# The first batch's output projection moved to the end of the attention block

## The reference, cut to what matters

```python
q, k, v = (xn @ Wq.T + bq) * SCALE, xn @ Wk.T + bk, xn @ Wv.T + bv      # 16 heads of 16
probs = softmax(einsum('bqhd,bkhd->bhqk', q, k))                          # 4096 x 4096 for each head
attn = einsum('bhqk,bkhd->bqhd', probs, v).reshape(b, s, d) @ Wo.T + bo
ffn = sum over 8 experts of weight(xn) * ((silu(xn @ Wg) * (xn @ Wu)) @ Wd)
return x + attn + ffn
```

## Time and profile before

| | us |
|---|---|
| median of three runs | 6645.73 |
| lowest, highest run | 6642.88, 6661.02 |
| the profiled execution's own time | 6664.44 |
| its span | 6662.7 |
| output phase | 6583.84 to 6662.7 |

### The profile page before, as it was taken

One profiled execution on the slowest core, in us unless ns is written; L12 is line 12 of the kernel. 1 busy time (PEld: TensorE's weight loads), 2 busy tenths in 40 slices (PEclk: granted clock), 3 DMA queues, 4 the chain that ended last, 5 costly groups with the idle time before them and its releaser, 6 DMA issues. The chain is left out here.

```text
span 6662.7 us, 158241 instructions
## 1 busy us (share of the span) xinstructions
PE 6493.2 (97%) x57104; PEld 3100.8 (47%) x57104; DVE 5738.7 (86%) x6163; ACT 4968.8 (75%) x9045; POOL 518.2 (8%) x543
## 2 busy tenths in 40 slices
PE   7999999979999999999999999999999999999996
PEld 6888888833333333333333333333333333333334
DVE  4554554479999999999999999999999999999982
ACT  3333333318888888888888888888888888888884
POOL 2222222200000000000000000000000000000000
PEclk9999999969999999999999999999999999999998
DMA  2111111121111111111111111111111111111104
GB/s 94 45 45 45 45 45 45 39 34 26 32 34 33 30 29 29 29 30 29 30 30 29 30 29 30 29 29 29 32 32 32 32 32 33 34 31 29 29 10 159
DMA packets 248804, 248.24 MB, mean 37 GB/s; under 512 B 167848, under 2 KB 208552, under 8 KB 241704
## 3 DMA queue, kind: packets, MB, share of 16 engines
q1 hardware_dynamic: 235872, 202.88, 13.8%
q0 software_dynamic: 12176, 35.14, 2.2%
HBM read 159.26 MB, written 76.58 MB: 35 GB/s over the span
## 5 line engine op out<-in xcount | busy, mean ns | idle before, releaser
L904 DVE TENSOR_REDUCE mx<-sc 128x1 f32<-128x1024 f32 x4096 | 5001.7, 1223 | 91.0 <-PE sc L797 33.4
L891 ACT ACTIVATE pr<-st 128x512 f32<-128x512 f32 x8120 | 4413.8, 597 | 620.8 <-PE st L811 594.4
L820 PE MATMUL pv<-pr,vst 128*32 128x256 f32 x32768 | 2611.8, 391 | 23.3 <-ACT oT L880 15.3
L811 PE MATMUL st<-experts 50*128 50x512 f32 x8120 | 2041.4, 499 | 4.6 <-ACT pr L891 3.0
L797 PE MATMUL sc<-experts 48*128 48x512 f32 x8192 | 1672.4, 405 | 36.4 <-DVE mx L904 27.7
L811 PEld LDWEIGHTS st<-experts 50*128 50x128 f32 x8120 | 757.3, 183 | 1675.5 <-ACT pr L891 1668.7
L820 PEld LDWEIGHTS pv<-pr,vst 128*32 128x32 f32 x32768 | 648.2, 108 | 1545.2 <-ACT pr L891 784.8
L797 PEld LDWEIGHTS sc<-experts 48*128 48x128 f32 x8192 | 788.8, 189 | 77.0 <-DVE mx L904 66.2
L432 ACT ACTIVATE gated<-gate 128x512 f32<-128x512 f32 x256 | 152.2, 599 | 631.2 <-PE up L75 631.0
L602 DVE TENSOR_TENSOR hraw<-gated,up 128x512 f32<-128x512 f32 x256 | 173.2, 686 | 431.2 <-ACT gated L432 428.0
L75 PE MATMUL gate<-xT,experts 128*128 128x512 f32 x1536 | 407.6, 402 | 10.5 <-issue 10.5
(11 more groups left out here) (101 smaller groups left out, 1279.4 us busy)
## 6 DMA issues: line engine op xcount, KB each, us to landing
experts<-parts_d SPq DMA_DIRECT2D x372, 256.0 KB, 4.3
parts_d<-part SPq DMA_DIRECT2D x64, 512.0 KB, 3.0
x_in<-in_L_attn_hidden_states SPq DMA_DIRECT2D x16, 512.0 KB, 4.6
v_d<-v_sb SPq DMA_DIRECT2D x32, 256.0 KB, 2.2
vst<-v_d SPq DMA_DIRECT2D x128, 64.0 KB, 2.2
experts<-turned SPq DMA_DIRECT2D x512, 4.0 KB
sums_d<-oT SPq DMA_DIRECT2D x256, 32.0 KB
whole<-sums_d POOLq DMA_DIRECT2D x32, 256.0 KB, 2.9
```

Source lines behind the costliest of these rows:

```text
L811: nc.tensor.matmul(score_bank(at, x + grp), kr[par][r0:r0 + ROWSM, kb * P:(kb + 1) * P], qr[par][r0:r0 + ROWSM, q0:q0 + GT], start=True, s ...
L820: last = nc.tensor.matmul(pv[VC * j:VC * (j + 1), cols], vst[par][:, kb, :], pr[:, (QSUB * kb + j) % PRING, cols], start=(kb == 0 and half ...
L891: nc.scalar.activation(pr[:, (QSUB * kb + j) % PRING, :], score_bank(2 * at + q, x), ACT.Exp).then_inc(st_read, 1)
L904: nc.vector.reduce_max(mx[par][:, u // MAXU, u % MAXU:u % MAXU + 1], sc[g % 2][:, :], AX.X).then_inc(sc_read, 1)
```

## The change

Groups 0 to 7 of the output, which are the first batch's, are taken inside the attention's block. Groups 8 to 15 stay in the output phase, whose loops now run over 8 groups.

- Loads. In pass 61 (`q == 1`) SP issues 16 loads of 256 KB, the first batch's whole `attn_d`, into a third of the `experts` buffers that the attention does not use. In pass 62 (`q == 2`) it issues 8 loads of 256 KB, the base of groups 0 to 3, into four new `early_base` tiles. Each load waits for a count of `pv_done`, one load for each 1.5 key blocks.
- Compute. Behind the last values' product PE has the 8 groups' matmuls, with `sc` as accumulators; ACT has their high parts behind the last `sums_kept`; DVE has the low parts of groups 0 and 1 ahead of the last head's `inverted`, and the rest behind it. The high and low parts lie in `kept_rows(c, 0)`, the rows of the even heads; the sums of base and product are written to `pr`.
- Stores. Behind the last `sums`, SP waits for each group's sum, reloads `early_base` for groups 4 to 7, and stores the group. SP ends the block when all eight have landed.

The core of the diff, in which the output phase's other loops change in the same way as those shown:

```diff
@@ attention_phase, names
+        o_base = [sb(f"early_base{i}", [P, TPG, D], F32) for i in range(HELD)]
...
+        def o_attn(g):
+            flat = c.experts[g // HELD][:, 2, :, :, :].rearrange("p e k i -> p (e k i)")
+            return flat[:, g % HELD * KC * GT:(g % HELD + 1) * KC * GT].bitcast(F32).rearrange("p (k t) -> p k t", t=GT)
+        def o_attT(g, hl):
+            return kept_rows(c, 0)[g % 2][:, hl * KC * GT:(hl + 1) * KC * GT].rearrange("p (k t) -> p k t", t=GT)
+        def o_out(g):
+            return pr[:, 2 * g:2 * g + 2, :].rearrange("p s (u d) -> p (s u) d", d=D)
@@ sync
+            def early(piece):
+                g, half = divmod(piece, 2)
+                if g < GPB:
+                    sp.dma_start(o_attn(g)[:, half, :], c.attn_d[half * P:(half + 1) * P, g * GT:(g + 1) * GT]).then_inc(o_attn_in, DMA)
+                else:
+                    g -= GPB
+                    sp.dma_start(o_base[g][:, 2 * half:2 * half + 2, :], rows_of(c.base_d, g)[:, 2 * half:2 * half + 2, :]).then_inc(o_base_in, DMA)
...
                     ending = last and q // 2 == heads - 1
+                    if last and q in (1, 2):
+                        sp.wait_ge(attn_stored, H * DMA)
+                        for piece in range(2 * GPB) if q == 1 else range(2 * GPB, 2 * GPB + 2 * HELD):
+                            wait_alone(sp, pv_done, s * KB + PV_PRE + 1 + QK_EVERY * (piece % (2 * GPB)) // 2, passed)
+                            early(piece)
...
             in_turn(body)
+            for g in range(GPB):
+                wait_alone(sp, o_sum, g + 1, passed)
+                if g + HELD < GPB:
+                    sp.dma_start(o_base[g][:, :, :], rows_of(c.base_d, g + HELD)).then_inc(o_base_again[g], DMA)
+                sp.dma_start(rows_of(a["out"], g), o_out(g)).then_inc(o_stored, DMA)
             sp.wait_ge(sums_stored, (SUPERS * SUM_STORES + 1) * DMA)
+            sp.wait_ge(o_stored, GPB * DMA)
@@ tensor
                 times_v(SUPERS - 1, KB - 1, RING - 1, half)
+            for g in range(GPB):
+                pe.wait_ge(o_low, (g + 1) * KC)
+                if g >= 2:
+                    pe.wait_ge(o_sum, g - 1)
+                for t in range(TPG):
+                    last = product(nc, sc[g % 2][:, t * D:(t + 1) * D], [[o_attT(g, hl)[:, k, t * P:(t + 1) * P] for hl in range(2)] for k in range(KC)],
+                                   [[v[:, k, :] for v in c.woT] for k in range(KC)])
+                last.then_inc(o_full, 1)
@@ scalar
             sums_kept(SUPERS - 1)
+            act.wait_ge(o_attn_in, 2 * GPB * DMA)
+            for g in range(GPB):
+                if g >= 2:
+                    act.wait_ge(o_full, g - 1)
+                for k in range(KC):
+                    nc.scalar.activation(o_attT(g, 0)[:, k, :], o_attn(g)[:, k, :], ACT.Identity).then_inc(o_high, 1)
@@ vector
+            early_low(0)
+            early_low(1)
             inverted(HEADS - 1)
+            dve.wait_ge(o_base_in, 2 * HELD * DMA)
+            for g in range(GPB):
+                dve.wait_ge(o_full, g + 1)
+                if g >= HELD:
+                    dve.wait_ge(o_base_again[g - HELD], DMA)
+                for i in range(2):
+                    ins = nc.vector.tensor_tensor(o_out(g)[:, 2 * i:2 * i + 2, :], sc[g % 2][:, i * GT:(i + 1) * GT].rearrange("p (t d) -> p t d", d=D),
+                                                  o_base[g % HELD][:, 2 * i:2 * i + 2, :], ALU.add)
+                ins.then_inc(o_sum, 1)
+                if g + 2 < GPB:
+                    early_low(g + 2)
@@ output_phase, sync
-            for g in range(NG):
-                i, b, c0 = g % DEEP, g // GPB, (g % GPB) * GT
+            for g in range(GPB):
+                i, b, c0 = g % DEEP, 1, g * GT
```

More of the change, by code:

```diff
@@ L40 @@
 RING = 2
+HELD = 4
 ORDER = ((0, 1, 0), (0, 0, 1))
@@ L654, in attention_phase @@
         attn_stored = sem("attn_stored")
+        o_attn_in = sem("early_attn_in")
+        o_base_in = sem("early_base_in")
+        o_base_again = [sem(f"early_base_again{i}") for i in range(HELD)]
+        o_high = sem("early_high")
+        o_low = sem("early_low")
+        o_full = sem("early_full")
+        o_sum = sem("early_sum")
+        o_stored = sem("early_stored")
         passed = sem("passed_a")
@@ L690, in attention_phase, with rows_of @@
         WHEN_IN = {0: (0, 1), UNITS // 2: (2,), UNITS: (3,)}
+        def o_attn(g):
[5 more added lines that the diff above has]
+            return pr[:, 2 * g:2 * g + 2, :].rearrange("p s (u d) -> p (s u) d", d=D)
+        def rows_of(dram, g):
+            return dram[g * GT:(g + 1) * GT, :].rearrange("(t p) d -> p t d", p=P)
         def first_order(g):
@@ L964, in _, with early_low @@
             counted(dve, body)
-            inverted(HEADS - 1)
+            def early_low(g):
+                if g >= 2:
+                    dve.wait_ge(o_full, g - 1)
+                for k in range(KC):
+                    dve.wait_ge(o_high, g * KC + k + 1)
+                    nc.vector.tensor_tensor(o_attT(g, 1)[:, k, :], o_attn(g)[:, k, :], o_attT(g, 0)[:, k, :].bitcast(F32), ALU.subtract).then_inc(o_low, 1)
+            early_low(0)
+            early_low(1)
+            inverted(HEADS - 1)
+            dve.wait_ge(o_base_in, 2 * HELD * DMA)
[9 more added lines that the diff above has]
+                    early_low(g + 2)
 def output_phase(nc, a, c):
@@ L997, in _ @@
                     sp.wait_ge(stored[i], (g // DEEP) * DMA)
-                sp.dma_start(base[i][:, :, :], tokens_of(c.base_d, g)).then_inc(base_in[i], DMA)
+                sp.dma_start(base[i][:, :, :], tokens_of(c.base_d, GPB + g)).then_inc(base_in[i], DMA)
             for i in range(DEEP):
-                sp.wait_ge(stored[i], (NG // DEEP) * DMA)
+                sp.wait_ge(stored[i], (GPB // DEEP) * DMA)
         @block.gpsimd
         def _(pool):
-            for g in range(NG):
+            for g in range(GPB):
                 pool.wait_ge(sum_ready, g + 1)
-                nc.gpsimd.dma_start(tokens_of(a["out"], g), base[g % DEEP][:, :, :]).then_inc(stored[g % DEEP], DMA)
+                nc.gpsimd.dma_start(tokens_of(a["out"], GPB + g), base[g % DEEP][:, :, :]).then_inc(stored[g % DEEP], DMA)
         @block.tensor
         def _(pe):
-            for g in range(NG):
+            for g in range(GPB):
                 pe.wait_ge(low_ready, (g + 1) * KC)
@@ L1038, in _ @@
             low(0)
-            for g in range(NG):
-                if g + 1 < NG:
+            for g in range(GPB):
+                if g + 1 < GPB:
                     low(g + 1)
```

## The result

Five runs of each kernel: the changed one 6622.15 us (median; 6618.49 to 6627.22), the kernel before 6657.05 (6642.88 to 6661.02). The ratio of the two, over all runs, is 0.9959, 95% interval 0.9948 to 0.9969, so about 27 us less, and anything from 21 to 35; the two medians alone differ by 34.9. The forecast had 6622.7 us and 23.1 us less. That the absolute time is hit to 0.6 us is luck. The forecast was taken from the median of three runs of before, 6645.73; from that of all five, 6657.05, the same gain gives 6634.

A forecast was written before the change was run, and what follows sets the result against it. Bounds: the last division with PE idle, POOL's DRAIN at the barrier, then a transfer-limited output phase. Barrier at 6594.65 plus 44.98 gives 6639.6 against 6662.7, 23.1 us less; on the median 6645.73 that is 6622.7, range 6614 to 6632.

The forecast's parts named there:

- Loads under the attention, 0: Passes 61 and 62: 16 and 8 loads of 256 KB from SP delay no engine, cost 0.
- The barrier 10.8 us later: End of the attention's block: with the early groups the output phase starts at 6594.65 instead of 6583.84.
- The last store's landing: End of the early groups: SP's last store takes 3.5 us to land, ends 2.5 and 6.1.
- POOL's DRAIN hidden: Attention's end: beside the groups, division stored at 6586.7, DRAIN over at 6590.9, before 6594.3; its 4.15 us leave the path.
- Rival A: Attention's end: slowed division transfers end the block, output phase 6 us later than forecast, 17 us gained, 6628.7; chance 0.10.
- a fixed price of POOL's: Barrier behind the attention: POOL's DRAIN takes 4.15 us, 4.11 at the program's end, shared by no other engine.
- The half output phase, 44.98: Remaining output phase: its first half as it ran, 40.69, plus the ending, 4.29; ends 43.0 and 46.0 us.
- So here the transfers are the limit: Output phase: a group's 1.57 MB takes 4.7 us at 335 GB/s, against 2.87 us of PE.
- The other half, 33.88: Output phase's second half: loads and stores of eight groups go, 33.88 us removed.
- PE's clock is the only thing in the rows that varies of itself: Whole execution: said beside the runs' spread of 18.1 us, nearly the size of the gain.
- Rival D: Whole execution: groups run as forecast, but the clock elsewhere moves medians by as much, 6640 or so; chance 0.07.
- Rival B: Early groups: SP's stores move at half rate, start 14 us later than forecast, 9 us gained, 6636.7; chance 0.08.

The follow-up runs named there:

- the loads alone: The kernel before plus the 24 early loads and the new tiles and semaphores, with nothing reading them: ratio 0.9999 to the kernel before, output phase 81.1 us.
- with 8 buffers: The changed kernel with 8 buffers instead of 4 for each load in the output phase: ratio 0.9962 to the kernel before, output phase 40.8 us.
- before, again: The kernel before, unedited, run and profiled once more: ratio 0.9999 of itself, output phase 83.6 us.
- the last experiment: Changed kernel, 8 buffers per output-phase load, bases of groups 8 to 11 loaded in the attention's last pass: ratio to before 0.9951, again 0.9946.

## Why the prediction was right

The sign and the mechanism held, and the gain is within the interval. The three profiles of the changed kernel show each part of the sum where it was put; the hit on the absolute time is luck, as said above. Term by term:

- *Loads under the attention, 0.* Shown by the loads alone.
- *The barrier 10.8 us later.* It is 10.1 in the first profiles. In the means it is 32.3 (changed, three profiles) against 22.2 (before twice and the loads alone), 10.1 again. The parts: PE starts 2.6 us after its last product (forecast 2.7); the first sum follows the reciprocal; 2.87 us a group. The last store's landing was too dear: from the end of the last sum at 6577.65 to SP at 6580.7 is 3.05 us, for 3.6.
- *POOL's DRAIN hidden.* It ended 1.3 us before SP in the first profile and 3.6 in the second; the forecast had 3.4. POOL's two waits that meet SP's traffic were 7.8 (from issue to the multiply) and 6.2, for 6.7 and 6.1. Rival A wasn't far: a chain 1.3 us longer would have set the barrier. As "a fixed price of POOL's" the DRAIN held for the attention's block alone; at the program's end it was 4.11 before and 3.73 in the changed kernel.
- *The half output phase, 44.98.* 43.5 to 44.3; no later loads stand beside its last groups. "So here the transfers are the limit" was too strong: with 8 buffers the same bytes took 3 us less. The sum didn't need it, since it took the half phase as it ran.
- *The other half, 33.88.* This is the mis-sized term. The sum took it from one execution, and that one was short: in `before, again` it is 38.05 (stores of group 7 and the last three, below), with the loads alone 36.2. With the whole phase's mean of 81.2 us (these three profiles) the account is 81.2 - 43.8 - 10.1 = 27.3, and the ratio says 27. The forecast's 23 lies in the interval too, so it is the stretches that say 27, and from a phase that spread over 4.7 us in three profiles.

```profile
6627.63 0.75 POOL L1006 DMA_DIRECT2D out<-o_base  x1 [2.12 <-DVE o_base L1045]
...
6653.77 0.75 POOL L1006 DMA_DIRECT2D out<-o_base  x1 [2.57 <-DVE o_base L1045]
6660.87 0.75 POOL L1006 DMA_DIRECT2D out<-o_base  x1 [6.35 <-DVE o_base L1045]
6665.68 0.75 POOL L1006 DMA_DIRECT2D out<-o_base  x1 [4.06 <-DVE o_base L1045]
```

POOL's waits for the last two sums were 6.35 and 4.06 us, in the first profile 4.33 and 2.56. The chain of `before, again` says what they stand for, and its timeline shows PE's last group:

```profile
6642.76 7.66 DMA out<-o_base
...
6650.44 0.37 SPq L998
...
6650.85 6.48 DMA attn<-attn_d
```

```profile
6659.43 4.63 PE L75 MATMUL ob<-woT,attT 128*128 128x256 f32 x24 [3.96 <-DVE attT L1035]
```

A store took 7.66 us to land, SP's base load waited for it, and the next attention tile behind that took 6.48 more: the first wait. The second is PE's last group, 4.63 us for the usual 2.87, at a granted clock of 0.50 (6660 to 6663). Why a transfer takes longer in one execution than in another stays open.

- *The rest of the spread.* "PE's clock is the only thing in the rows that varies of itself" was wrong. The clock does move the first copy, within a spread of 17 us over the twelve profiles, but the pace of the passes varies too, by 26.7, at a granted clock of 1.00, and the output phase by 4.7. Rival D was right in kind: single executions differ by as much as the gain. Over five runs it did not cover it.
- *The range.* Its lower end before the allowance is 6619.0 and not 6619.6; nothing hangs on it. It counts 5 us for the runs at each end, less than either spread above. Later runs of the changed kernel lay between 6622.76 and 6654.08, with the kernel before higher too; what repeats is the ratio.

Rival B is out: SP's stores of 512 KB left in step with PE, and the last landed in 3 us.

## What to carry to other kernels

A last phase that lives on loads is shortened by whatever can be loaded while the main loop uses the DMA engines little (0.16 of their time from 2000 to 6500 us in the kernel before): 6 MB here at no cost that shows, and 2 MB more in the last experiment, where 1.2 us of the attention stay unexplained. The price of work moved ahead of a barrier is what it adds behind the chain that already ends there, 10 us for 37 here, since the division and POOL's DRAIN cover the rest. Read each term of such a sum from more than one execution where there are several, and compare stretches rather than totals when the total carries a lottery of its size.

## What the runs showed of the hardware that was not expected

**Two paces of one loop.** Waits of ACT for PE's score tiles over two passes, first in the kernel before, then in the changed one (total, times, longest):

```profile
ACT pr L891 <- PE st L811: 19.6, 126, 0.2
```

```profile
ACT pr L944 <- PE st L856: 10.1, 64, 0.3
```

In the slow pace ACT waits once for every second tile, in every pass. In the fast one a pass with these waits, 79.68 us from copy to copy, and a pass of 78.86 without them take turns; the rows below are two passes of the changed kernel, one after the other.

```profile
ACT pr L944 <- PE st L856: 0.2, 1, 0.2
```

```profile
ACT pr L944 <- PE st L856: 9.9, 63, 0.3
```

Nothing in the loop's work differs. Profiles of the changed kernel had 3, 42 and 2 passes out of 63 at the slow pace, those of the kernel before 62 and 56, the last kernel 62 twice. What picks the pace was not tried, and whether a program can shift the odds stays open.

**POOL's DRAIN** at the end of the attention's block took 4147 or 4150 ns in all twelve profiles, whether POOL's last transfer was issued 2.5 us before it or 13. It is not one figure for every block: at the end of the program it took 3727 to 4112, at the end of the setup 2746 to 2751, of the token phase 6121 to 7067. What it depends on stays open.

**DVE and POOL hold each other up.** Where POOL's multiply met DVE's low parts, one of them was longer: the multiply 1.72 us against 1.26 before, or, in the kernel with 8 buffers, DVE's two low parts 2.38 against 1.28:

```profile
6557.22 2.38 DVE L1030 TENSOR_TENSOR experts<-experts 128x512 fp32r<-128x512 f32 x2
...
6557.72 1.32 POOL L825 TENSOR_TENSOR whole<-whole,recs 128x512 f32<-128x512 f32 x1 [5.36 <-DMA recs<-rden_d]
...
6559.65 2.54 PE L76 MATMUL sc<-woT,experts 128*128 128x256 f32 x19 [0.80 <-DVE experts L1030]
```

PE waited 0.80 us for it. The Trainium skill, page "SBUF — State Buffer", section "SBUF: two separate sides", says that the port pair which the two share is an exclusive lock: whichever starts first holds it for the whole instruction, and a DVE instruction with two SBUF inputs counts, though only against a GpSimd one that reads SBUF. With that rule the traces agree: a low part reads two SBUF tiles, and the second of the pair lasted 1.78 us, for its own 0.68 and the 1.22 that were left of POOL's.
